# A megakernel's routed expert loops: 23 tiles of 256 slots become 15 of 256 and 9 of 128, written out

## The chip, the cores and the metric

The program runs on one core of one Trainium2 chip. The metric is the device time of one execution in microseconds (us): the median of the runs of a kernel, and for comparisons the ratio to the kernel before on the same chip.

## The reference, cut to what matters

Four decoder layers of mixed kinds run over x of 16 x 128 tokens (2048 tokens) of width 256. The change touches the two layers whose feed-forward part routes each token to 2 of 8 experts:

```python
def moe(x, router_w, router_b, W1, b1, W2, b2, W3, b3):   # layer 0: D_FF = 1024, with biases
    logits = x @ router_w + router_b
    topv, topi = jax.lax.top_k(logits, TOP_K)
    topw = jax.nn.softmax(topv, axis=-1)
    ...
    h = h2 * jax.nn.silu(h1)          # h1 = x W1 + b1, h2 = x W2 + b2
    eo = jnp.einsum('ebsf,efd->ebsd', h, W3) + b3[:, None, None, :]
    return jnp.einsum('bse,ebsd->bsd', comb, eo)
```

Layer 1 has the same form with 512 hidden columns, no biases, sigmoid gating and one more expert that all tokens share. The kernel computes an expert only for the tokens that chose it: 4096 (token, choice) pairs in each of the two layers.

## The kernel before, in words

Each routed stage has two parts. `route` computes the logits, the two choices of each token, and how many tokens each expert has; it gives each pair a slot so that an expert's slots begin at a multiple of `SLOTS` = 256. With 4096 pairs and 8 experts that makes at most `ROUTED` = 23 tiles of 256 slots, 46 chunks of 128. VectorE builds all that in one chain of small steps (`c.step`, `c.wait`: the wait is for all steps before), writes the expert of each tile to `TE`, and, with one-hot matrices (`OA`, `OB`, `OV`) and TensorE, the tables `TOKEN` (which row goes to a slot) and `CHOICE` (where its result goes).

`expert_tiles` then runs over the tiles. A tile has NF chunks of 128 hidden columns, 8 in layer 0 and 4 in layer 1. I call the work on TensorE between `up(t, 0)` and `up(t+1, 0)` the turn of tile t; in it the engine alternates, chunk by chunk (a round), between `up` of tile t and `down` of tile t-1. Each product is made of three single passes (high x high, high x low, low x high) over numbers that are split in a high part of type fp32r and a rest:

- GpSimd (POOL) gathers 2 x 128 rows of a tile with `gather` (an indirect DMA for each 128), three tiles ahead. TensorE transposes them (`turn`), ScalarE and VectorE split them (`CH`, `CL`).
- SyncE (SP) loads a tile's expert weights: `U` (two matrices, 2 MB in layer 0 and 1 MB in layer 1) and `DN` (half as much), each into one of two buffers. For tile t it waits until `UL` of tile t-2 is made, issues `U`, then waits for `DL` of tile t-2 and issues `DN`. The register with the expert's number is loaded first.
- For each chunk ScalarE makes `UH` and `DH` (copies), VectorE makes `UL`, POOL makes `DL` (subtractions). The rings hold 4 chunks.
- `up` has the weights stationary and streams the tile's 256 columns: 12 matmuls of 256 columns for a chunk. `silu` (ScalarE) and `hidden` (VectorE, with bias in layer 0) make `HR`, split again to `HH` and `HL`.
- `down` has `HH`/`HL` stationary and streams 256 columns of `DH`/`DL`: 3 matmuls for each 128 slots, 6 for a chunk.
- The result is copied to `Y` and POOL scatters it with `put`, an indirect DMA for each 128 slots. Offsets for `gather` and `put` are first copied to a small tile `AT`, by POOL and ScalarE.

Each engine's loop is a hardware loop over pairs of tiles (`turns`, line 1464), with the first and the last tiles written out. POOL's order within tile t is DL(0), the copy to `AT`, DL(1), gather of t+3, DL(2) ..., and at chunk `PUT` (4 in layer 0, 3 in layer 1) the put of tile t-1. In layer 0 part of the next layer's keys and values (`kv`) fills TensorE while `route` waits.

Of the kernel before, what the change touches and what calls it, by code (L numbers as in the profile page):

```python
# [39 lines left out]
ROUTED = (2 * T + 8 * (SLOTS - 1)) // SLOTS  # L40


C_IDENT, C_DECAY, C_COS, C_SIN, C_CAUSAL, C_LESS, C_HEAD, C_IOTA, C_END = (
    0, 128, 256, 384, 512, 640, 768, 776, 792)


def shape_constants():
# [15 lines left out]
    c[:, C_IOTA:C_IOTA + 16] = np.arange(16)[None, :]  # L63
    return c
# [16 lines left out]
def build(nc, I, out):  # L81
# [20 lines left out]
    with top:  # L102
# [12 lines left out]
        YT = nc.dram_tensor("results_by_choice", (2 * T + ROUTED * SLOTS, D), F32, kind="Internal").ap()  # L115
# [1008 lines left out]
        def route(tag, RW, bias_rows, gating, gate, W12, ROWS, TAB, TE, expert_tiles, weights, fill=None):  # L1124
# [4 lines left out]
            with ExitStack() as c:  # L1129
# [9 lines left out]
                ST = sb_in(c, f"{tag}_ST", [P, 3, E8])  # L1139
                G = sb_in(c, f"{tag}_G", [P, 3, B])  # L1140
                SL = sb_in(c, f"{tag}_SL", [P, 2, B, E8])
                CMP = sb_in(c, f"{tag}_CMP", [P, expert_tiles, E8 - 1])
                TEF = sb_in(c, f"{tag}_TEF", [P, expert_tiles])
                IOTA_T = sb_in(c, f"{tag}_IOTA_T", [P, expert_tiles])
# [23 lines left out]
                with nc.Block() as block:  # L1168
# [34 lines left out]
                    def _(pool):  # L1203
                        nc.gpsimd.iota(IOTA_T[:, :], pattern=[[1, expert_tiles]], base=0, channel_multiplier=0,
# [34 lines left out]
                    def _(dve):  # L1239
# [42 lines left out]
                        while lag < B:  # L1282
# [6 lines left out]
                        c.step(nc.vector.tensor_scalar(CNT[:, :], SUMS[:, at, B - 1, :], float(SLOTS - 1), None, ALU.add))  # L1289
                        c.wait()  # L1290
                        c.step(nc.vector.tensor_scalar(CNT[:, :], CNT[:, :], SLOTS.bit_length() - 1, None,
                                                       ALU.logical_shift_right))
                        c.wait()
                        c.step(nc.vector.tensor_copy(ST[:, 0, :], CNT[:, :]))
                        c.wait()
                        src, lag = 0, 1
                        while lag < E8:
                            c.step(nc.vector.tensor_copy(ST[:, 1 + (src == 1), 0:lag], ST[:, src, 0:lag]))
                            c.step(nc.vector.tensor_tensor(ST[:, 1 + (src == 1), lag:E8], ST[:, src, lag:E8],
                                                           ST[:, src, 0:E8 - lag], ALU.add))  # L1300
                            c.wait()
                            src, lag = 1 + (src == 1), 2 * lag
                        first_tile = 3 - src
                        c.step(nc.vector.tensor_tensor(ST[:, first_tile, :], ST[:, src, :], ST[:, 0, :], ALU.subtract))
                        c.step(nc.vector.tensor_tensor(SUMS[:, 1 - at, :, :], SUMS[:, at, :, :], sums, ALU.subtract))
                        c.wait()
                        c.step(nc.vector.tensor_tensor(SUMS[:, 1 - at, :, :], SUMS[:, 1 - at, :, :], rank, ALU.add))
                        c.step(nc.vector.tensor_scalar(ST[:, 0, :], ST[:, first_tile, :], float(SLOTS), None, ALU.mult))
                        c.step(nc.vector.tensor_tensor(
                            CMP[:, :, :],  # L1310
                            ST[:, first_tile, 1:E8].rearrange("p (o e) -> p o e", o=1).broadcast_to([P, expert_tiles, E8 - 1]),
                            IOTA_T[:, :].rearrange("p (t o) -> p t o", o=1).broadcast_to([P, expert_tiles, E8 - 1]),
                            ALU.is_le))
                        c.wait()
                        c.step(nc.vector.tensor_reduce(TEF[:, :], CMP[:, :, :], AX, ALU.add))
                        c.step(nc.vector.tensor_tensor(
                            SUMS[:, at, :, :], SUMS[:, 1 - at, :, :],
                            ST[:, 0, :].rearrange("p (o e) -> p o e", o=1).broadcast_to([P, B, E8]), ALU.add))
                        c.wait()
                        nc.vector.tensor_copy(TE[:, 0:expert_tiles], TEF[:, :]).then_inc(s_te, 1)  # L1320
# [8 lines left out]
                        c.step(nc.vector.tensor_copy(SI[:, :, :], G[:, 0:2, :]))  # L1329
                        c.wait()  # L1330
# [14 lines left out]

                        dve.wait_ge(s_tab, 1)
# [16 lines left out]
        class SlotTables:  # L1363


            CHUNKS = ROUTED * SLOTS // P

# [4 lines left out]
        class ExpertWeights:  # L1372


            def __init__(self, c, tag, FF, WUP, WDOWN, TE, bias):
# [3 lines left out]
                if bias:  # L1379
                    self.BU = sb_in(c, f"{tag}_BU", [P, 2, 2, FF // P])  # L1380

# [3 lines left out]
            def expert(self, sp, i, j):  # L1385
                return sp.value_load(self.TE[0:1, bass.ds(2 * i + j, 1)], min_val=0,
                                     max_val=self.WUP.shape[0] - 1)

            def up(self, sp, e, j):
                sp.dma_start(self.U[:, j, :, :, :], self.WUP[bass.ds(e, 1), :, :, :, :]  # L1390
                             .rearrange("o p k a f -> (o p) k a f")).then_inc(self.s_up[j], 16)

            def up_bias(self, sp, e, j):
                sp.dma_start(self.BU[:, j, :, :], self.bias[0][bass.ds(e, 1), :, :, :]
                             .rearrange("o p a f -> (o p) a f")).then_inc(self.s_up[j], 16)
# [12 lines left out]

        def expert_tiles(tag, weights, TAB, fill=None, place=None):

# [2281 lines left out]
```

## Time and profile before

| | us |
|---|---|
| median of 3 runs | 1662.16 |
| lowest and highest | 1660.51, 1671.48 |
| profiled execution, device time | 1667.93 |
| profiled execution, span of the trace | 1666.1 |
| of it TensorE busy | 1401.1 |

The profiled execution is one run. Its device time is 5.8 us above the median, and its span is 1.8 us shorter than its device time; what lies around the span is the start and end of the program. Busy time is the union of an engine's instructions, with modelled ends for matmuls.

### The profile page before, as it was taken

The page shows a single profiled execution, that of the slowest core. Times are in us where ns is not written, and L with a number is a line of the kernel's source. Part 1 is how long each engine was busy: PE and PEld are TensorE (multiplying, and loading weights), DVE is VectorE, ACT ScalarE, POOL GpSimd, SP SyncE. Part 2 cuts the span into 40 slices and gives each one's busy share as a digit, 9 for nine tenths or more (in the row PEclk, how much of TensorE's full clock was granted, in tenths as well). Part 3 has the DMA queues.
Part 4 walks back from the last instruction along what each step waited for, and adds up shares of the span by engine and source line. Part 5 has one row for each costly group of instructions (what it writes and reads, how often), then busy time and mean ns, then how long its engine had stood idle before and what let it go on. Part 6 is the DMA issues. An engine that isn't in the chain of part 4 may idle for free. (4 is left out here: it accounts for less than half of the span.)

```text
span 1666.1 us, 31746 instructions
## 1 busy us (share of the span) xinstructions
PE 1401.1 (84%) x10246; PEld 1189.0 (71%) x10246; DVE 1151.6 (69%) x2497; ACT 939.7 (56%) x2055; POOL 758.4 (46%) x813
## 2 busy tenths in 40 slices
PE   2799978999999999968986579999876976455898
PEld 0445565899999999944665579999875862244787
DVE  6357755688788788756965648778665758786554
ACT  3246642777777777746752338777624546563332
POOL 2223202466666666513321138888701760344444
PEclk8799987999999999979996789999998999675999
DMA  5000005365665665340012117667441000101001
GB/s 178 1 1 1 1 24 200 119 235 190 220 231 189 232 222 189 119 133 1 1 52 89 76 54 234 210 211 228 143 134 60 1 1 0 29 4 59 1 19 33
DMA packets 62367, 171.86 MB, mean 103 GB/s; under 512 B 11760, under 2 KB 43248, under 8 KB 53056
## 3 DMA queue, kind: packets, MB, share of 16 engines
q1 hardware_dynamic: 53440, 146.50, 25.3%
q0 software_dynamic: 8832, 24.13, 4.5%
q8 instruction: 55, 0.90, 0.2%
q14 instruction: 40, 0.33, 0.1%
HBM read 152.25 MB, written 18.35 MB: 102 GB/s over the span
## 5 line engine op out<-in xcount | busy, mean ns | idle before, releaser
L1749 POOL TENSOR_TENSOR l0m_e_DL<-l0m_e_DN,l0m_e_DH 128x256 fp32r<-128x256 f32 x184 | 180.9, 988 | 122.6 <-ACT l0m_e_DH L1588 74.9
L1532 PE MATMUL PS<-l0m_e_CH,l0m_e_UH 128*128 128x256 f32 x736 | 211.3, 287 | 1.9 <-DVE l0m_e_CL L1682 1.9
L1532 PE MATMUL PS<-l0m_e_CH,l0m_e_UL 128*128 128x256 f32 x736 | 209.5, 285 | 0.0
L1532 PE MATMUL PS<-l0m_e_CL,l0m_e_UH 128*128 128x256 f32 x736 | 209.4, 284 | 0.0
L1654 DVE TENSOR_TENSOR l0m_e_UL<-l0m_e_U,l0m_e_UH 128x512 fp32r<-128x512 f32 x184 | 149.0, 810 | 12.1 <-ACT l0m_e_UH L1579 12.1
L1532 PEld LDWEIGHTS PS<-l0m_e_CH,l0m_e_UH 128*128 128x128 f32 x736 | 142.3, 193 | 2.2 <-ACT l0m_e_UH L1579 2.2
L1532 PEld LDWEIGHTS PS<-l0m_e_CL,l0m_e_UH 128*128 128x128 f32 x736 | 142.2, 193 | 0.0
L1532 PEld LDWEIGHTS PS<-l0m_e_CH,l0m_e_UL 128*128 128x128 f32 x736 | 142.1, 193 | 0.0
L1666 DVE SCALAR_TENSOR_TENSOR Z<-PS,l0m_e_BU,Z 128x256 f32<-128x256 f32 x184 | 88.7, 482 | 73.3 <-ACT Z L1596 70.9
L1596 ACT ACTIVATE Z<-PS,l0m_e_BU 128x256 f32<-128x256 f32 x184 | 87.6, 476 | 83.3 <-PE PS L1532 83.3
L1579 ACT CAST l0m_e_UH<-l0m_e_U 128x512 fp32r<-128x512 f32 x184 | 113.0, 615 | 0.0
L1532 PE MATMUL PS<-l1m_e_CH,l1m_e_UH 128*128 128x256 f32 x368 | 107.7, 293 | 5.9 <-DVE l1m_e_CL L1682 5.9
L1548 PE MATMUL PS<-l0m_e_DH,l0m_e_HH 128*128 128x256 f32 x368 | 104.8, 285 | 2.8 <-issue 2.2
L1532 PE MATMUL PS<-l1m_e_CH,l1m_e_UL 128*128 128x256 f32 x368 | 105.1, 286 | 0.0
L1532 PE MATMUL PS<-l1m_e_CL,l1m_e_UH 128*128 128x256 f32 x368 | 105.1, 285 | 0.0
L1548 PE MATMUL PS<-l0m_e_DH,l0m_e_HL 128*128 128x256 f32 x368 | 104.7, 284 | 0.0
L1548 PE MATMUL PS<-l0m_e_DL,l0m_e_HH 128*128 128x256 f32 x368 | 104.6, 284 | 0.0
L1677 DVE TENSOR_TENSOR l0m_e_HL<-Z,l0m_e_HH 128x256 fp32r<-128x256 f32 x184 | 96.8, 526 | 0.1
L1749 POOL TENSOR_TENSOR l1m_e_DL<-l1m_e_DN,l1m_e_DH 128x256 fp32r<-128x256 f32 x92 | 87.1, 956 | 16.0 <-ACT l1m_e_DH L1588 12.7
L1654 DVE TENSOR_TENSOR l1m_e_UL<-l1m_e_U,l1m_e_UH 128x512 fp32r<-128x512 f32 x92 | 79.6, 866 | 21.4 <-ACT l1m_e_UH L1579 20.8
L3443 POOL TENSOR_TENSOR Z<-l3f_WI,Z 128x512 f32<-128x512 f32 x32 | 50.7, 1584 | 60.8 <-DVE Z L3539 55.7
L1532 PEld LDWEIGHTS PS<-l1m_e_CH,l1m_e_UH 128*128 128x128 f32 x368 | 71.5, 194 | 7.6 <-issue 4.9
(545 smaller groups left out, 4509.1 us busy)
## 6 DMA issues: line engine op xcount, KB each, us to landing
l0m_e_U<-in_l_up SPq DMA_DIRECT2D x23, 2048.0 KB
l0m_e_DN<-in_l_down SPq DMA_DIRECT2D x23, 1024.0 KB
l1m_e_U<-in_l_up SPq DMA_DIRECT2D x23, 1024.0 KB, 6.7
l1m_e_DN<-in_l_down SPq DMA_DIRECT2D x23, 512.0 KB, 3.9
CTX<-in_ctx SPq DMA_DIRECT2D x2, 2048.0 KB, 10.0
l1a_GA<-results_by_choice SPq DMA_DIRECT2D x16, 256.0 KB, 5.8
l1m_c_GA<-results_by_choice SPq DMA_DIRECT2D x16, 256.0 KB, 5.0
Z<-in_l_b_rows SPq DMA_DIRECT2D x23, 128.0 KB, 2.3
```

What stands on the lines that cost most here:

```text
L1532: ins = nc.tensor.matmul(hb(f)[:, a * SLOTS:(a + 1) * SLOTS], w[:, f % RING, k, a, :], x[:, j, k, :], start=(p == 0), stop=(p == len(passe ...
L1548: ins = nc.tensor.matmul(yb(j)[:, r * D:(r + 1) * D], h[:, j % 2, f, r * P:(r + 1) * P], w[:, f % RING, :], start=(f == 0 and r == 0 and p ...
L1579: nc.scalar.copy(UH[:, f % RING, :, :, :], U[:, j % 2, :, :, f * P:(f + 1) * P]).then_inc(s_uh, 1)
L1596: nc.scalar.activation(SG[:, f % RING, :], hb(f)[:, 0:SLOTS], ACT.Silu, **kw).then_inc(s_silu, 1)
L1654: nc.vector.tensor_tensor(UL[:, f % RING, :, :, :], U[:, j % 2, :, :, f * P:(f + 1) * P], UH[:, f % RING, :, :, :].bitcast(F32), ALU.subtr ...
L1666: ins = nc.vector.scalar_tensor_tensor(out=HR[:, f % RING, :], in0=second, scalar=BU[:, j, 1, f:f + 1], in1=SG[:, f % RING, :], op0=ALU.ad ...
L1677: nc.vector.tensor_tensor(HL[:, j % 2, f, :], HR[:, f % RING, :], HH[:, j % 2, f, :].bitcast(F32), ALU.subtract).then_inc(s_hl, 1)
L1749: nc.gpsimd.tensor_tensor(DL[:, f % RING, :], DN[:, j, f, :], DH[:, f % RING, :].bitcast(F32), ALU.subtract).then_inc(s_dl, 1)
L3443: nc.gpsimd.tensor_tensor(HR(u), HA(u), HB(u), ALU.add).then_inc(s_h, 1)
```

## The change: what it does

- An expert with n chunks of 128 slots gets n // 2 tiles of 256 and n % 2 of 128. There are 15 wide (B) and 9 narrow (S) tiles, 39 chunks; wide tiles that an input needs beyond 15 become two narrow ones each. All 24 run in a fixed order, BBSBBSBS three times. `route` computes two kinds of starts, two tables of experts and a slot by either kind, so its chain on VectorE is longer; its one-hot matrices have 39 columns in place of 46.
- A narrow tile has the rows stationary and streams 256 columns of weights: 6 matmuls of 256 columns for a chunk, for 128 slots. The output then has slots on partitions, so layer 0's bias comes from a seventh matmul (`PICK`, a one-hot column repeated, times `BROW`), and `HR` is transposed back by TensorE (`turn_hidden`, two transposes for each pair of chunks, a unit). `silu`, `hidden`, `HH` and `HL` take the two chunks of a unit at once. `down` has 3 matmuls for a chunk.
- The hardware loops are gone: all tiles are written out, and `gather` and `put` read the tables without `AT`.
- In layer 0 a 128 x 256 array of biases is loaded and split by POOL ahead of `route`.

```diff
-ROUTED = (2 * T + 8 * (SLOTS - 1)) // SLOTS
+WIDE, NARROW = 15, 9
+ROUTED = WIDE + NARROW
+CHUNKS = 2 * WIDE + NARROW
+TILE_KINDS = "BBSBBSBS" * 3
...
+            units = [(t, f) for t in range(tiles) for f in (range(NF) if big(t) else range(0, NF, 2))]
...
+                if not big(t):
+                    turn_at.setdefault(divmod(NF * t + f + 2, NF), []).append(u)
+                split_at.setdefault(divmod(NF * t + f + (1 if big(t) else 3), NF), []).append(u)
...
-                def turns(eng, body):
-
-
-                    for j in range(2):
-                        body(0, j)
-                    with eng.Fori(1, pairs - 1) as i:
-                        for j in range(2):
-                            body(i, j)
...
+                                half = hb(u)[:, (f % 2) * 2 * P:(f % 2 + 1) * 2 * P]
                                 for p, (w, x, k) in enumerate(passes):
...
+                                    ins = nc.tensor.matmul(half, x[:, t % 2, k, 0:P],
+                                                           w[:, f % RING, k, :, :].rearrange("p a n -> p (a n)"),
+                                                           start=(p == 0), stop=(not bias and p == len(passes) - 1),
                                                            skip_group_check=True)
+                                if bias:
+                                    s = small_index(t)
+                                    ins = nc.tensor.matmul(half, PICK[:, s, f:f + 1].broadcast_to([P, P]), BROW[:, :],
+                                                           start=False, stop=True, skip_group_check=True)
                             ins.then_inc(s_up_done, 1)
...
+                        def turn_hidden(u):
+                            pe.wait_ge(s_hr, u + 1)
+                            for h in range(2):
+                                ins = nc.tensor.transpose(pair(hb(u))[:, h, 0:P], HR[:, u % 4, h * P:(h + 1) * P], IDENT)
+                            ins.then_inc(s_ht, 1)
...
+                        for t in range(tiles + 1):
+                            for f in range(NF):
+                                if t < tiles:
+                                    up(t, f)
+                                if t >= 1:
+                                    down(t - 1, f)
+                                for u in turn_at.get((t, f), ()):
+                                    turn_hidden(u)
+                                if f == NF // 2 and t + 1 < tiles:
+                                    turn(t + 1)
...
+                                up_high(count(t, f) + 2)
+                                down_high(count(t - 1, f) + 2)
+                                for u in split_at.get((t, f), ()):
+                                    hidden_high(u)
+                                if t < tiles and ends(t, f):
+                                    silu(at_unit[t, f])
...
+                                pool.wait_ge(s_dh, count(t, f) + 1)
+                                nc.gpsimd.tensor_tensor(DL[:, f % RING, :], DN[:, t % 2, f, :],
                                                         DH[:, f % RING, :].bitcast(F32), ALU.subtract).then_inc(s_dl, 1)
...
+                                if f == 1 and t + 3 < tiles:
+                                    gather(t + 3)
+                                if f == PUT and t >= 1:
+                                    put(t - 1)
```

## Rows read from the trace of the kernel before

**Rows 1.** The page's head table: busy us, share of the span, instructions.

```profile
PE 1401.1 (84%) x10246; PEld 1189.0 (71%) x10246; DVE 1151.6 (69%) x2497; ACT 939.7 (56%) x2055; POOL 758.4 (46%) x813
```

**Rows 2.** Windows, the two tile loops: length, engines as in Rows 1, PEclk, DMA, GB/s.

```profile
301.00:713.30 412.30, 409.51 (x3400) 408.88 (x3398) 328.47 (x594) 306.59 (x778) 268.50 (x289) 0.99 0.54 195
984.00:1205.50 221.50, 214.60 (x1744) 211.12 (x1744) 171.98 (x296) 161.51 (x431) 184.79 (x197) 0.99 0.62 199
```

**Rows 3.** Timeline of SP's DMA issues in layer 0: start, us, queue.

```profile
399.21 0.33 SPq L1398 DMA_DIRECT2D l0m_e_DN<-in_l_down  x1
400.45 0.34 SPq L1390 DMA_DIRECT2D l0m_e_U<-in_l_up  x1
...
416.93 0.33 SPq L1398 DMA_DIRECT2D l0m_e_DN<-in_l_down  x1
418.48 0.34 SPq L1390 DMA_DIRECT2D l0m_e_U<-in_l_up  x1
```

**Rows 4.** Timeline of PE in layer 0: matmuls one behind another, and a turn.

```profile
407.13 0.28 PE L1532 MATMUL PS<-l0m_e_CH,l0m_e_UH 128*128 128x256 f32 x1
...
408.09 0.28 PE L1532 MATMUL PS<-l0m_e_CH,l0m_e_UL 128*128 128x256 f32 x1
...
519.89 0.60 PE L1516 MATMUL PS<-CONST,l0m_e_ROW 128*128 128x128 f32 x4
```

**Rows 5.** Groups of POOL, layer 1, 1040 to 1183 us: busy, mean ns | idle before.

```profile
L1749 POOL TENSOR_TENSOR l1m_e_DL<-l1m_e_DN,l1m_e_DH 128x256 fp32r<-128x256 f32 x60 | 58.2, 978 | 3.0 <-POOL l1m_e_AT L1723 2.1 <-ACT l1m_e_DH L1588 0.3
L1734 POOL DMA_INDIRECT results_by_choice<-l1m_e_place,l1m_e_AT x30 | 32.6, 1088 | 7.1 <-issue 6.8 <-PE PS L1516 0.3
L1727 POOL DMA_INDIRECT l1m_e_ROW<-rows_by_token,l1m_e_AT x30 | 31.1, 1036 | 6.9 <-issue 6.0 <-ACT l1m_e_place L1618 0.6
L1723 POOL COPY l1m_e_AT<-l1m_TOKEN 128x2 uint32 x14 | 6.9, 490 | 0.0
```

**Rows 6.** Windows of one turn in layer 0, split where the weights have landed.

```profile
399.20:411.00 11.80, 11.80 (x101) 11.80 (x100) 9.31 (x18) 8.74 (x24) 7.73 (x9) 1.00 0.83 300
411.00:416.90 5.90, 5.90 (x52) 5.90 (x51) 5.16 (x9) 4.66 (x12) 4.20 (x5) 1.00 0.13 45
```

**Rows 7.** Waits, layer 1's loop: us in total, times, longest.

```profile
ACT l1m_e_UH L1579 <- DMA l1m_e_U<-in_l_up: 20.7, 14, 3.1
...
PE PS L1532 <- DVE l1m_e_CL L1682: 5.9, 8, 1.5
```

**Rows 8.** Groups of DVE, then ACT, layer 0, 400 to 680 us.

```profile
L1654 DVE TENSOR_TENSOR l0m_e_UL<-l0m_e_U,l0m_e_UH 128x512 fp32r<-128x512 f32 x127 | 103.6, 816 | 0.0
L1677 DVE TENSOR_TENSOR l0m_e_HL<-Z,l0m_e_HH 128x256 fp32r<-128x256 f32 x127 | 66.5, 524 | 0.0
L1666 DVE SCALAR_TENSOR_TENSOR Z<-PS,l0m_e_BU,Z 128x256 f32<-128x256 f32 x127 | 61.2, 482 | 50.8 <-ACT Z L1596 49.1
...
L1596 ACT ACTIVATE Z<-PS,l0m_e_BU 128x256 f32<-128x256 f32 x127 | 60.4, 476 | 58.6 <-PE PS L1532 58.6
```

**Rows 9.** Timeline of layer 0's route: DVE's chain, and the one-hots behind it.

```profile
270.55 0.17 DVE L1289 TENSOR_SCALAR l0m_r_CNT<-l0m_r_SUMS 128x8 int32<-128x8 f32 x1
...
272.05 0.28 DVE L1305 TENSOR_TENSOR l0m_r_SUMS<-l0m_r_SUMS,PS 128x128 f32<-128x128 f32 x1
272.37 0.29 DVE L1307 TENSOR_TENSOR l0m_r_SUMS<-l0m_r_SUMS,PS 128x128 f32<-128x128 f32 x1
...
273.55 0.18 DVE L1320 CAST l0m_TE<-l0m_r_TEF 128x23 int32<-128x23 f32 x1
...
281.54 1.14 DVE L1341 TENSOR_TENSOR l0m_r_OA<-l0m_r_BLK,l0m_r_AB 128x368 bf16<-128x368 f32 x1
...
284.61 0.49 PE L1189 MATMUL PS<-l0m_r_OV,l0m_r_OB 128*128 128x92 bf16 x8 [0.76 <-POOL l0m_r_OV L1215]
```

**Rows 10.** The page's table of DMA issues: KB each, us to landing.

```profile
l1m_e_U<-in_l_up SPq DMA_DIRECT2D x23, 1024.0 KB, 6.7
```

**Rows 11.** The page's DMA queue table, instruction fetches: packets, MB, share.

```profile
q8 instruction: 55, 0.90, 0.2%
```

More of the change, by code:

```diff
@@ L1552, in down @@
                                                            skip_group_check=True)
                             ins.then_inc(s_y, 1)
-                        def tile(i, j):
-                            for f in range(NF):
-                                up(i, j, f)
-                                if begun(i, j, 1):
-                                    down(i, j - 1, f)
-                                if f == NF // 2 and exists(i, j + 1):
-                                    turn(i, j + 1)
                         if fill is not None:
@@ L1564, in _ @@
                             fill.end(pe)
-                        turn(0, 0)
-                        turns(pe, tile)
-                        for f in range(NF):
-                            down(*LAST, f)
+                        turn(0)
+                        for t in range(tiles + 1):
[8 more added lines that the diff above has]
+                                    turn(t + 1)
@@ new lines, in _ @@
+                        up_high(1)
+                        cols_high(0)
+                        for t in range(tiles + 1):
+                            for f in range(NF):
+                                if not bias and f == 1 and t >= 2:
+                                    out_rows(t - 2)
+                                up_high(count(t, f) + 2)
[4 more added lines that the diff above has]
+                                    silu(at_unit[t, f])
+                                if f == NF // 2 and t + 1 < tiles:
+                                    cols_high(t + 1)
@@ new lines, in _ @@
+                        up_low(0)
+                        up_low(1)
+                        cols_low(0)
+                        for t in range(tiles + 1):
+                            for f in range(NF):
+                                up_low(count(t, f) + 2)
+                                if t < tiles and ends(t, f):
+                                    hidden(at_unit[t, f])
+                                for u in split_at.get((t, f), ()):
+                                    hidden_low(u)
+                                if bias and f == 1 and t >= 2:
+                                    out_rows(t - 2)
+                                if f == NF // 2 and t + 1 < tiles:
+                                    cols_low(t + 1)
```

590 lines of the change are left out of this document (310 added, 280 removed).

## The prediction

> **What bounds the kernel now.** The page's head table comes first [rows 1]: TensorE is busy for 84% of the span, more than any other engine, but that is an average over stages. The windows of the two tile loops say more [rows 2]. They are 412.3 and 221.5 us long, 38% of the span, and TensorE is busy for 409.5 and 214.6 us of them at a granted clock of 0.99, the upper of its two levels (2.4 GHz).
>
> Busy time hides how fast the engine steps, so the timeline is next. Matmuls of 256 columns start 0.12 us apart (407.13 to 408.09 with seven between, eight steps of 0.12), though each is shown as 0.28 us long [rows 4]. In layer 0, SP issues `DN` every 17.72 us [rows 3], and that is a turn of TensorE: 144 matmuls x 0.12 = 17.28 us, and 4 transposes for the rest, 0.11 us each. The first and last starts (399.21, 416.93) are one such period, and 23 turns of 17.72 are 407.6 of the 412.3 us. So layer 0's loop is TensorE's alone, with nothing lost at the back edge of the hardware loop.
>
> Layer 1 is another case. Its matmuls and transposes, 1656 x 0.12 + 92 x 0.11 = 208.8 us, leave 12.7 us of the window. POOL's groups between 1040 and 1183 us [rows 5] sum to 128.8 us busy (58.2 + 32.6 + 31.1 + 6.9) and 17.0 idle before them: all 143 us, with overlaps. POOL never waits there for more than a gap. Fifteen tiles in 143 us are 9.5 us each, where TensorE needs 36 x 2 x 0.12 + 0.44 = 9.1. POOL is the second bound, by 5%. Late `DL` holds SP's `DN` issue and the `U` issue behind it, which is where ScalarE's 20.7 us of waits for `U` come from [rows 7].
>
> **Layer 0's loop.** A wide tile keeps its 144 matmuls and 4 transposes. A narrow one has 8 x (6 + 1) for `up`, 8 x 3 for `down`, so 80 matmuls, and 2 + 8 transposes. Before: 23 x 144 = 3312 matmuls and 92 transposes, 397.4 + 10.1 = 407.5 us. After: 15 x 144 + 9 x 80 = 2880 and 78 + 72 = 150, 345.6 + 16.5 = 362.1 us. That is 45.4 us less if TensorE stays the bound. The bias matmul has a stationary operand that repeats one column; no row shows such a load, so I take the 0.12 us of the others. Its bounds are 0 (72 matmuls hidden: 8.6 us better) and the 0.28 of an unpipelined one (72 x 0.16 = 11.5 us worse); all 736 x 3 `up` matmuls of the loop step at 0.12, which is why I take that. For `turn_hidden` the same two bounds lie between 0 and the 0.60 us that four transposes took together with their latency [rows 4], and I stay at 0.11.
>
> What could be late instead in the shorter turns? There are three lengths: wide behind wide 17.7 us, wide behind narrow (120 matmuls) 14.8, narrow behind wide (104 matmuls, 12 transposes) 13.8.
> - *Weights.* `DN` and `U`, 3 MB, move at 300 GB/s and a share of 0.83 in the 11.8 us behind the `DN` issue; in the 5.9 us left of the turn there are 45 GB/s [rows 6]. So they have landed about 10.6 us behind the `U` issue (400.45 to 411). `UH(0)` of the next tile is asked for in round 6 of 8, in a narrow turn 6 x 1.7 = 10.2 us from its start, and `U` is issued about 2 us before that start: 12.2 us against 10.6. It fits, with two more rounds before TensorE itself needs it.
> - *VectorE.* A full round costs it 816 + 524 + 482 ns by mean durations [rows 8], 1.82 us against 1.80 of TensorE where a wide tile follows a narrow one. The window's union is less, 328.5 us for 184 rounds, 1.79 with `CL` and `Y` in it [rows 2]. It sits at the edge in 8 of 24 turns and is idle in the narrow ones (0.82 + half of 1.0 against 1.67), and the rings let it lag by two rounds.
> - *POOL.* 1.02 us a round and four indirect DMAs of 1.3 at most, 13.3 us against 13.8 in the worst turn, 11 to 12 in most.
> I charge 2.5 us for these edges: 43 us saved, 34 to 46 as bounds.
>
> **The new chain in a narrow tile.** TensorE goes from the end of a unit's second `up` to its `turn_hidden` through 19 matmuls in layer 0 (6 + 7 + 6) and 18 in layer 1, 2.2 us. In that time ScalarE makes `silu` (0.48) and VectorE `hidden` (0.48) [rows 8]; in the worst case VectorE has just begun a stretched `UL` (0.82). That is 1.8 us and some 0.2 for four hand-overs, so it is covered by about 0.2 us at worst and by 1 us as a rule. Behind a waiting TensorE would stand the next `up`, and behind that all. Price at zero, up to 0.3 us for half of the 54 units (8 us) as a bound. `HL` of a narrow unit is three rounds late instead of one; `down` needs it a turn later.
>
> **Layer 1's loop.** TensorE: 15 x 72 + 9 x 36 = 1404 matmuls, 78 + 36 transposes, 168.5 + 12.5 = 181.0 us, 27.8 less than 208.8. POOL: a `DL` costs (58.2 + 3.0) / 60 = 1.02 us, an indirect DMA (32.6 + 7.1 + 31.1 + 6.9) / 60 = 1.295, a copy to `AT` 0.49 [rows 5]. Before: 92 x 1.02 + 92 x 1.295 + 23 x 0.49 = 224.2 us. After: 96 `DL` (one tile more), 78 indirect DMAs, no copy: 97.9 + 101.0 = 198.9 us. POOL saves 25.3 us and stays ahead of TensorE's 181 by 10%, so POOL sets this loop and the saving is 25 us. `U`, 1 MB, takes 6.7 us to land [rows 10]; a narrow turn lasts 6.7 and a wide one behind it 7.7 against POOL's mean of 8.3, so the load has as much room as before. Bounds: 35 us if POOL's pace falls away as a bound (181 + the 5 us that every loop has at its end, against 221.5), 10 us if each `U` behind a narrow turn is late by the longest wait seen, 3.1 us [rows 7], at half of the 9.
>
> A rule on POOL bears on this. The rows show `UL` at 816 ns and `HL` at 524 in the mean, both of two SBUF operands, while `hidden` and `CL`, which read PSUM, keep their times; `HL` of a narrow tile reads PSUM. The Trainium skill (GPSIMD Engine Reference, in its table of the engine's facts) says that GpSimd's SBUF interfaces contend with VectorE instructions that have two SBUF inputs. By that rule `DL` gets shorter beside narrow tiles, where half of such work is gone; by the rows alone its mean stays. The sum keeps the mean.
>
> **Loops written out.** Every engine now streams new instructions through both loops. The page shows 55 instruction fetches of 16 KB on one queue, 0.2% of the DMA share [rows 11], and the written-out first and last tiles of layer 0 have the same turn as those inside. I price it at 0; a bound is 1 us for each of some 30 more fetches if none is ahead of its use. The Trainium skill (Runtime: NRT & Kernel Launch, Instruction fetch mechanics) says that a taken branch out of the current window costs a fetch stall and that straight code is fetched ahead. By its first half the loops would gain from the edit; the equal turns of [rows 3] show no such stall to win back.
>
> **Route.** Both routes get a longer chain. From 270.55 to 273.55 there are nine groups of steps with a wait behind each, 3.1 us; a step of 128 x 128 with its wait takes 0.32 (272.05 to 272.37), small ones 0.07 to 0.2 [rows 9]. After it there are fourteen groups, and by the same prices (0.21 + 0.29 + 0.20, three scans of 0.27, then 0.85, 0.75, 0.65, 0.65, 0.45, 0.50, 0.40, 0.40) 6.2 us: 3.1 more. The one-hots shrink by 46 to 39 columns: `OA` at 1.14 us [rows 9] becomes 0.97, three times, and `OV` behind the last, about 0.8 us less in all. The chain ends each route (TensorE waits at 284.61 for it), and layer 0's keys and values come behind it, so 2.3 us more in each: 4.6. Loading and splitting the biases lies beside the transposes ahead of the route: 0. The first `gather` of layer 1 no longer waits for a copy (0.6), and each stage ends in one store fewer; against that I set 1 us for turns that don't average out.
>
> **Sum.** -43 - 25 + 4.6 = -63, and with 3 us for small waits that I have not seen -60. Against the profiled execution, 1667.9 us, that is 1608; it was 5.8 above the median, so against the median of 1662.2 it is 1602.
>
> **Rivals.**
> 1. *Forecast*, 1602 (1592 to 1613), chance 0.55.
> 2. *Layer 1 becomes load-bound and layer 0 VectorE-bound* (the two lower bounds): -34 - 10 + 4.6 = -39, 1623. For it speaks that both rates are within a tenth of their edge; against it that the mean loads leave room. 0.22.
> 3. *POOL lets go*: its `DL` falls to its uncontended time and TensorE sets layer 1: -45 - 35 + 4.6 = -75, 1587. 0.14.
> 4. *The new hand-overs stall TensorE*, slower than before: at each of the 54 units TensorE waits for `silu` and `hidden` because ScalarE or VectorE stands at an earlier wait in its order. It eats the gain from 1.1 us a unit; at 1.5 us it is -60 + 81, 1683. Against it is the cover of 2.2 us. 0.05.
> 5. *No change* (the narrow turns as long as wide ones, because loads take 17 us a tile): the 5.9 us of near idle DMA [rows 6] speak against it. 0.04, 1660.
>
> The predicted time is 1602. The range takes in 1 to 3 and leaves out the last two and the ends: 1584 to 1628. A measurement here tells about 1% (17 us) from no change: faster 0.91, within 1% 0.05, slower 0.04.
>
> **What would show it.** Turns of 17.7, 14.8 and 13.8 us in layer 0 and TensorE still without gaps; in layer 1 POOL without idle time at a mean of 8.3 us a tile; route's chain 2.3 us longer. Wrong would be: waits of PE for `HR` or `UH`, `UL` waits on DMA in layer 0, an instruction fetch in front of a gap, a clock below 0.99 in the loops.

## The result, and the profile after

The changed kernel takes 1604.84 us in the median (1603.77 to 1607.69, 4 runs), against 1666.82 us for the kernel before on the same chip: a ratio of 0.963, with a 95% interval of 0.958 to 0.968. The forecast was 1602; it started from the 1662.16 us of three runs of the kernel before, and a fourth (1675.46) has moved that median. The saving is 62.0 us, where 60 was forecast. The profiled execution took 1603.92 us, its span is 1602.1.

First the page's head table and two of its rows for DMA, those that answer to [rows 1], [rows 10] and [rows 11]; then the windows of the two loops (columns as in [rows 2]).

```profile
PE 1324.1 (83%) x9624; PEld 1110.0 (69%) x9642; DVE 1130.4 (71%) x2469; ACT 906.0 (57%) x1952; POOL 728.4 (45%) x753
...
q8 instruction: 81, 1.33, 0.4%
...
l1m_e_U<-in_l_up SPq DMA_DIRECT2D x24, 1024.0 KB, 6.4
```

```profile
299.10:668.10 369.00, 364.83 (x3026) 363.20 (x3026) 315.55 (x548) 285.70 (x717) 261.41 (x264) 0.99 0.59 224
940.60:1142.00 201.40, 188.57 (x1514) 183.67 (x1514) 158.07 (x273) 149.89 (x392) 160.64 (x168) 0.99 0.64 219
```

The reader is to see two unlike loops. In layer 0 TensorE is still busy for all but 4 us. In layer 1 it is now idle for 13 us of 201, and POOL, which [rows 2] have at 184.8 of 221.5, stands at 160.6 of 201.4: no engine fills that loop. By the starts and ends of the two loops in the trace (first matmul of `up`, last one of `down`) the spans divide like this:

| stretch | before | after | difference |
|---|---|---|---|
| up to layer 0's loop | 300.7 | 299.1 | -1.6 |
| layer 0's loop | 412.6 | 369.0 | -43.6 |
| between the loops | 270.7 | 272.5 | +1.8 |
| layer 1's loop | 221.4 | 201.4 | -20.0 |
| behind it | 460.6 | 460.1 | -0.5 |

So all of the gain is in the loops, 43.6 where 43 was forecast and 20.0 where 25 was.

**Layer 0.** The timeline of PE shows how it steps now (start, us, engine, line, tiles, form):

```profile
332.25 0.28 PE L1588 MATMUL PS<-l0m_e_UL,l0m_e_CH 128*128 128x256 f32 x1
332.37 0.28 PE L1594 MATMUL PS<-l0m_e_BROW,l0m_e_PICK 128*128 128x256 f32 x1
332.49 0.28 PE L1614 MATMUL PS<-l0m_e_DH,l0m_e_HH 128*128 128x256 f32 x1
...
409.09 0.36 PE L1614 MATMUL PS<-l0m_e_DH,l0m_e_HH 128*128 128x256 f32 x1 [0.61 <-issue]
...
409.76 0.29 PE L1614 MATMUL PS<-l0m_e_DH,l0m_e_HL 128*128 128x256 f32 x1
409.88 0.38 PE L1601 MATMUL PS<-CONST,Z 128*128 128x128 f32 x2
410.02 0.36 PE L1588 MATMUL PS<-l0m_e_UH,l0m_e_CH 128*128 128x256 f32 x1
410.22 0.28 PE L1588 MATMUL PS<-l0m_e_UH,l0m_e_CL 128*128 128x256 f32 x1
```

The bias matmul takes a step of 0.12 us like its neighbours, as the forecast priced it. The two transposes of `turn_hidden` (the row of `Z`) cost 0.22 us together, also as priced: the matmul behind them starts 0.14 us after them, but its own step is 0.20 (410.02 to 410.22), so from 409.76 to 410.22 there are 0.46 us, of which two steps of 0.12 are the matmuls'. From the first matmul of each tile to that of the next the trace has 17.49 us for wide behind wide, 15.04 or 14.82 for wide behind narrow, 13.45 for narrow behind wide, and 14.3 where the tile before that wide one was narrow too: there (the 0.89 us from a start at 408.20 to 409.09) TensorE's weight load waits up to 0.8 us for the high part of the down weights.

**Layer 1.** The waits of its loop (us in total, times, longest) answer to [rows 7]; behind them stand POOL's groups from 960 to 1130 us, which answer to [rows 5].

```profile
POOL l1m_e_DL L1812 <- ACT l1m_e_DH L1655: 24.4, 24, 6.6
ACT l1m_e_UH L1645 <- DMA l1m_e_U<-in_l_up: 18.5, 15, 2.5
...
PEld PS L1581 <- ACT l1m_e_UH L1645: 6.3, 5, 1.9
PE PS L1581 <- DVE l1m_e_CL L1755: 6.2, 7, 1.5
```

```profile
L1812 POOL TENSOR_TENSOR l1m_e_DL<-l1m_e_DN,l1m_e_DH 128x256 fp32r<-128x256 f32 x82 | 73.6, 909 | 12.8 <-ACT l1m_e_DH L1655 11.7
L1801 POOL DMA_INDIRECT results_by_choice<-l1m_e_place,l1m_CHOICE x35 | 36.2, 1035 | 7.7 <-issue 7.7
L1792 POOL DMA_INDIRECT l1m_e_ROW<-rows_by_token,l1m_TOKEN x31 | 33.9, 1095 | 6.6 <-issue 5.9
```

POOL now stands idle ahead of `DL` for 12.8 us in this stretch, 11.7 of them waiting for `DH`, so it doesn't set the pace alone. TensorE waits for `CL` and `UH`. Why those are late is seen in the timeline of one start of a tile, all engines:

```profile
1005.02 0.35 SPq L1444 DMA_DIRECT2D l1m_e_U<-in_l_up  x1
```

```profile
1012.47 0.62 ACT L1645 CAST l1m_e_UH<-l1m_e_U 128x512 fp32r<-128x512 f32 x1 [2.14 <-DMA l1m_e_U<-in_l_up]
...
1013.19 0.69 DVE L1720 TENSOR_TENSOR l1m_e_UL<-l1m_e_U,l1m_e_UH 128x512 fp32r<-128x512 f32 x1 [1.74 <-ACT l1m_e_UH L1645]
...
1013.81 0.28 PE L1614 MATMUL PS<-l1m_e_DH,l1m_e_HL 128*128 128x256 f32 x1
1013.88 0.58 ACT L1684 CAST l1m_e_CH<-PS 128x512 fp32r<-128x512 f32 x1
...
1014.69 0.68 DVE L1755 TENSOR_TENSOR l1m_e_CL<-PS,l1m_e_CH 128x512 fp32r<-128x512 f32 x1
...
1015.63 0.36 PE L1581 MATMUL PS<-l1m_e_CH,l1m_e_UH 128*128 128x256 f32 x1 [1.54 <-DVE l1m_e_CL L1755]
```

ScalarE stands at `UH` of the next tile until its weights land (1012.4). TensorE has transposed that tile's rows by 1012.3, but `CH` comes behind `UH`, `DH`, `HH` and `silu` in its order, and VectorE's `CL` behind `UL`, `hidden` and `HL`. TensorE has nothing between 1014.1 and 1015.6. That is the theory of the experiments below: **the order on ScalarE and VectorE, with CH and CL behind the wait for the next weights**. Its rivals are the landing of `U` itself and POOL's pace, which the forecast had taken for the bound.

### The profile page after: what moved, and what is told of

The parts are those of the page before. It is cut to its first block and busy times, and to the rows that moved or that the text cites. A ratio compares the mean times of both kernels' runs of the same rounds, so it can differ in the third digit from the quotient of the medians.

```text
span 1602.1 us, 28284 instructions
## 1 busy us (share of the span) xinstructions
PE 1324.1 (83%) x9624; PEld 1110.0 (69%) x9642; DVE 1130.4 (71%) x2469; ACT 906.0 (57%) x1952; POOL 728.4 (45%) x753
## 5 line engine op out<-in xcount | busy, mean ns | idle before, releaser
L1720 DVE TENSOR_TENSOR l0m_e_UL<-l0m_e_U,l0m_e_UH 128x512 fp32r<-128x512 f32 x192 | 164.5, 862 | 10.7 <-ACT l0m_e_UH L1645 10.4
L1581 PE MATMUL PS<-l0m_e_CH,l0m_e_UH 128*128 128x256 f32 x480 | 138.5, 289 | 2.0 <-DVE l0m_e_CL L1755 2.0
L1581 PE MATMUL PS<-l0m_e_CH,l0m_e_UL 128*128 128x256 f32 x480 | 136.5, 284 | 0.0
L1581 PE MATMUL PS<-l0m_e_CL,l0m_e_UH 128*128 128x256 f32 x480 | 136.4, 284 | 0.0
L1581 PEld LDWEIGHTS PS<-l0m_e_CH,l0m_e_UH 128*128 128x128 f32 x480 | 92.8, 193 | 2.2 <-ACT l0m_e_UH L1645 2.2
L1581 PEld LDWEIGHTS PS<-l0m_e_CL,l0m_e_UH 128*128 128x128 f32 x480 | 92.9, 194 | 0.0
L1581 PEld LDWEIGHTS PS<-l0m_e_CH,l0m_e_UL 128*128 128x128 f32 x480 | 92.7, 193 | 0.0
L1655 ACT CAST l0m_e_DH<-l0m_e_DN 128x256 fp32r<-128x256 f32 x192 | 78.1, 408 | 0.2 <-PE PS L1614 0.2
L1581 PE MATMUL PS<-l1m_e_CH,l1m_e_UH 128*128 128x256 f32 x240 | 71.8, 299 | 7.7 <-DVE l1m_e_CL L1755 6.2
L525 POOL TENSOR_TENSOR l0a_KBD<-l0a_KT,CONST 128x512 f32<-128x512 f32 x32 | 33.4, 1046 | 91.3 <-PE PS L548 62.6
L1645 ACT CAST l1m_e_UH<-l1m_e_U 128x512 fp32r<-128x512 f32 x96 | 59.7, 623 | 24.6 <-DMA l1m_e_U<-in_l_up 18.5
```

Of the source, the lines that this page charges most:

```text
L525: nc.gpsimd.tensor_tensor(KBD[:, h % KR, :, :], KT[:, chunk, b * S:(b + 1) * S].rearrange("p (o s) -> p o s", o=1) .broadcast_to([P, 4, S] ...
L1581: ins = nc.tensor.matmul(hb(u)[:, a * SLOTS:(a + 1) * SLOTS], w[:, f % RING, k, a, :], x[:, t % 2, k, :], start=(p == 0), stop=(p == len(p ...
L1645: nc.scalar.copy(UH[:, f % RING, :, :, :], U[:, t % 2, :, :, f * P:(f + 1) * P]).then_inc(s_uh, 1)
L1655: nc.scalar.copy(DH[:, f % RING, :], DN[:, t % 2, f, :]).then_inc(s_dh, 1)
L1720: nc.vector.tensor_tensor(UL[:, f % RING, :, :, :], U[:, t % 2, :, :, f * P:(f + 1) * P], UH[:, f % RING, :, :, :].bitcast(F32), ALU.subtr ...
```

## The experiments

The move that several of them make is called the early turn: in layer 1 alone, the rows of the next tile are transposed and split in rounds 0 and 1, not in round 2, where ScalarE and VectorE already ask for the next tile's weights. Losses are read from the length of the loops in the trace, since the times of single runs of one kernel differ by up to 22 us. How well such a length repeats is seen where an edit leaves the loop alone: layer 0's loop is 368.9 or 369.0 us in seven traces (after, e3 to e6, e9, e12), and layer 1's is 201.4 in the kernel after and 201.3 in e7. Each kernel has one trace.

**e1_loops_out: the kernel before with its hardware loops written out.**

```diff
-                    with eng.Fori(1, pairs - 1) as i:
+                    for i in range(1, pairs - 1):
```

> The kernel before with its hardware loops written out and nothing else (23 wide tiles, the copies to AT stay). Theory A (the forecast: streaming new instructions costs nothing, the back edge cost nothing): the time of before, within 0.3%, layer 0's loop 412 us with turns of 17.7, layer 1's 221. Rival (instruction fetches are late): 10 to 30 us slower, with gaps in front of TensorE's instructions that nothing else ends. Rival (the back edge and the register arithmetic cost something): 3 us or more faster, layer 1's loop under 218.

1661.8 us, ratio 0.997 (0.994 to 1.001). Layer 0's loop 413.4 (before 412.6), layer 1's 216.0 (before 221.4). So 5 us of layer 1's gain came with this part here, none of layer 0's; e10 and e11 show that they aren't the loops' own cost.

**e2_old_form: the kernel after, but narrow tiles in the wide tiles' form**, weights stationary and 128 columns streamed, no `turn_hidden`, no bias matmul.

```diff
-            big = lambda t: KIND[t] == "B"
+            big = lambda t: True
...
-w[:, f % RING, k, a, :], x[:, t % 2, k, :],
+w[:, f % RING, k, a, :], x[:, t % 2, k, 0:W(t)],
```

> The changed kernel with the 9 narrow tiles in the wide tiles' form: weights stationary, 12 matmuls of 128 columns for a chunk, no turn back, no bias matmul. If a matmul's step goes by its columns (0.06 us for 128): a narrow tile of layer 0 takes 96 x 0.06 + 24 x 0.12 = 8.6 us in place of 10.7, 1 to 2% faster than the changed kernel if ScalarE and VectorE keep up. If the step has a floor near 0.12 us, as a load of 128 columns of weights for each matmul suggests: 14.6 us a narrow tile, layer 0's loop 35 us longer (404), layer 1's up to 19 us longer, 1640 to 1655 us in all. I expect a floor between, 0.08 to 0.12.

1644.66 us, ratio 0.985 (0.979 to 0.991), loops 396.1 (404 expected for a floor near 0.12 us) and 210.0. The timeline of PE in a narrow tile's turn says why half the columns save so little:

```profile
335.62 0.27 PE L1582 MATMUL PS<-l0m_e_CH,l0m_e_UL 128*128 128x128 f32 x1
335.73 0.27 PE L1582 MATMUL PS<-l0m_e_CH,l0m_e_UH 128*128 128x128 f32 x1
335.84 0.27 PE L1582 MATMUL PS<-l0m_e_CL,l0m_e_UH 128*128 128x128 f32 x1
```

A matmul of 128 columns with a new stationary operand takes a step of 0.11 us, where 256 columns take 0.12. What pays is fewer matmuls, and the streamed weights halve those of `up`. That form is worth 27.1 us of the 43.6 in layer 0 and 8.6 of the 20.0 in layer 1.

**e3_up_first: layer 1's SP issues the next tile's `U` ahead of this tile's `DN`.**

```diff
+                        for t in range(2, tiles + 1) if not bias else ():
+                            if t < tiles:
+                                e = weights.expert(sp, t)
+                                sp.wait_ge(s_ul, count(t - 1, 0))
+                                weights.up(sp, e, t)
+                            if t >= 3:
+                                sp.wait_ge(s_dl, count(t - 2, 0))
+                                weights.down(sp, before, t - 1)
+                            before = e
```

> In layer 1 SP issues U of tile t+1 ahead of DN of tile t, so that U no longer stands behind SP's wait for DL, which POOL makes; all else as in the changed kernel. Theory O (POOL's lateness reaches TensorE through SP's order): ScalarE's waits for U (18.5 us) fall to under 6 and layer 1's loop from 201 to 190 to 195 us. Theory P (POOL's own pace sets the loop, by whatever way): it stays at 199 to 203, and waits for DL or DH take the place of those for U. Theory L (the landing of 1.5 MB a tile sets it): 199 to 203 as well, with ScalarE's waits now for DN.

1600.27 us, ratio 0.958 (0.955 to 0.961). Layer 1's loop is 199.1, 2.3 less. `U` lands in 5.1 us in place of 6.4 and ScalarE's waits for it are gone from the list, yet the loop is in the range of theories P and L: `DN` lands in 6.0 us, where it took 3.9, and `CH` now waits for TensorE's transposes instead (20.7 us in the loop).

**e4_no_put_l1: the kernel after without layer 1's 39 scatters**, so that the results of that stage's routed part are not stored.

```diff
-                            if t >= 2:
-                                act.wait_ge(s_store[t % 2], rows_upto(t - 2))
...
                         def put(t):
+                            if not bias:
+                                return
                             pool.wait_ge(s_ycopy, t + 1)
```

> Layer 1's routed results are not stored (its 39 scatters are left out; what the layer adds is then not its experts' output), which takes 39 x 1.3 = 50 us of POOL's work away. Theory P or O (POOL's lateness sets layer 1's loop): it falls from 201 to 186 to 190 us, TensorE's 181 and its end; SP's issues of U come 2 us or more earlier in each tile. Theory L (landing of the weights): it stays above 196.

ScalarE's waits for the stores go with them. 1606.75 us (one run), layer 1's loop 197.6, where 186 to 190 was expected if POOL sets it. POOL is busy for 42 us less and the loop is 3.8 shorter, so in this kernel POOL's pace is a small part of the 20 us by which the loop stands above TensorE's 181.

**e5_turn_first: the early turn.** The condition changes so at three places, for TensorE (round 0), ScalarE and VectorE (round 1):

```diff
-                                if f == NF // 2 and t + 1 < tiles:
+                                if f == (NF // 2 if bias else 1) and t + 1 < tiles:
                                     cols_low(t + 1)
```

> The kernel after the change, with one move in layer 1's loop: the turn of the next tile's second tensors goes to the first round of a tile, and the copies of the combine weights' high and low halves (CH on ScalarE, CL on VectorE) to the second, so that they no longer stand in program order behind the up-cast of the next tile (UH), which waits for its weights to land. In the trace of the kernel after, TensorE starts on the next tile about 3.0 us after its up weights land, and 1.5 us of that is the wait for CL. Theory A (order on ScalarE and VectorE behind the landing is what layer 1 lost against its forecast): about 1.5 us less at each of some seven to ten starts of a tile, layer 1's loop from 201.4 to 188 to 194 us, the whole about 1592 to 1599. Theory B (the landing itself, or GpSimd's pace, sets it): the loop stays at 199 to 203 us, the whole at 1602 to 1607. Layer 0's loop stays at 369 us by both.

1600.0 us, ratio 0.960 (0.956 to 0.963), layer 1's loop 196.8: 4.6 less. The waits of PE for `CL` are gone but for one of 1.5 us, but the gain is less than the 7 to 13 expected. Theory A's range (188 to 194) and theory B's (199 to 203) both missed it; 12 waits of ScalarE for `U` are left between 960 and 1130 us. (The expectation calls `CH` and `CL` parts of combine weights. They are the high and low parts of the next tile's transposed rows.)

**e6_turn_first_up_first: e3 and e5 together.**

> The move of e5 and that of e3 together: CH and CL ahead of the next tile's up-cast, and layer 1's up weights of the next tile issued ahead of the down weights of this one. By theory A both waits at a tile's start are gone and what stays is the down weights' own landing: loop of layer 1 188 to 194 us, the whole 1590 to 1598. If the down weights' landing, which e3 made late, is as costly as the wait that e3 removed, it is e3 again: 199 us, the whole about 1600. Worse than e3 only if both moves delay the down side: 202 us or more.

1594.76 us (1591.45 to 1599.54), ratio 0.957 (0.955 to 0.960), loop 192.7: 8.7 less, more than the 2.3 and 4.6 of the single moves. It has the lowest median of the kernels here that compute everything. It ran on another chip than the kernel after, and the ratios, 0.957 and 0.963, have intervals that overlap (0.955 to 0.960, 0.958 to 0.968), so the gain is shown by the loop and not by the whole time.

**e7_no_bias_mm: the kernel after without the narrow tiles' bias matmul**, so their first products lack the bias.

```diff
-                                if bias:
-                                    s = small_index(t)
-                                    ins = nc.tensor.matmul(half, PICK[:, s, f:f + 1].broadcast_to([P, P]), BROW[:, :],
```

> The kernel after, with the narrow tiles' bias matmul left out (72 in each layer; their tiles' results lack the bias). The forecast priced these at 0.12 us each on TensorE's path in layer 0: 8.6 us, so layer 0's loop goes from 369 to 360 to 361 us, and layer 1's by 0 to 9 us, less than that where weights are waited for. If the loop stays within 2 us of 369, they lay beside other work, and the 43 us of layer 0 are made up otherwise than the forecast had it.

1600.47 us (one run), layer 0's loop 362.5, 6.5 less, not 8.6. Six of the nine turns are 0.7 to 0.9 us shorter (12.57 to 12.73 for 13.45), those of 14.3 by 0.53 only (13.77). TensorE's path pays the 0.12 us of a bias matmul where it isn't waiting for `DH` already; its weight loads wait 2.8 us for `DH` in place of 2.2. Layer 1 has no bias and no such matmul, against what the expectation says; its loop is 201.3, unchanged.

**e8_narrow_last: the 15 wide tiles first, then the 9 narrow ones.**

```diff
-TILE_KINDS = "BBSBBSBS" * 3
+TILE_KINDS = "B" * 15 + "S" * 9
```

> The kernel after, with the 9 narrow tiles behind the 15 wide ones in both loops rather than spread among them. TensorE's work is the same (sum of the turns within 3 us). A narrow tile behind a narrow one offers about 10.7 us of matmuls in layer 0 (80 by 0.12 us and what lies beside) to some 10.6 to 12 us of weights. If spreading them is what hides the weights, layer 0's loop grows by 5 to 15 us to 374 to 384, and layer 1's (6.7 to 7.7 us of matmuls for 9 us or more of transfers in each of nine tiles) by 5 to 20. If the order doesn't matter, both stay within 3 us of 369 and 201.

1612.09 us (one run), loops 375.3 and 205.5: 6.3 and 4.1 more. In layer 0 narrow behind narrow takes 11.1 to 12.0 us for some 10.7 of matmuls and transposes (80 x 0.12 + 4 x 0.22 + 0.22), in layer 1 7.3 to 8.7 for some 5.0. Here is such a start:

```profile
1095.86 0.62 ACT L1645 CAST l1m_e_UH<-l1m_e_U 128x512 fp32r<-128x512 f32 x1 [1.94 <-DMA l1m_e_U<-in_l_up]
1096.38 0.40 ACT L1655 CAST l1m_e_DH<-l1m_e_DN 128x256 fp32r<-128x256 f32 x1
1096.69 0.36 ACT L1684 CAST l1m_e_CH<-PS 128x256 fp32r<-128x256 f32 x1
```

```profile
1097.86 0.36 PE L1588 MATMUL PS<-l1m_e_UH,l1m_e_CH 128*128 128x256 f32 x1 [0.90 <-DVE l1m_e_CL L1755]
```

Spreading the narrow tiles hides weights, and is worth 10 us. In layer 1 the 4.1 us are a little under the 5 to 20 expected: its wide tiles, now all together, run at 9.07 us. Here are twelve of their turns, and POOL's largest group in them:

```profile
966.50:1075.30 108.80, 108.80 (x914) 108.80 (x913) 97.28 (x156) 85.03 (x218) 93.77 (x96) 1.00 0.68 230
```

```profile
L1812 POOL TENSOR_TENSOR l1m_e_DL<-l1m_e_DN,l1m_e_DH 128x256 fp32r<-128x256 f32 x49 | 45.1, 927 | 7.0 <-ACT l1m_e_DH L1655 6.5
```

TensorE has no idle time in them, though `CH` and `CL` stand in the old order. Beside the wide tiles of e1, some of which start late, what is missing here is above all the copies to `AT`. That limits the theory of the order, and comes back with e11.

**e9_expert_early: e5, and SP reads the next expert's number before it waits for `DL`.**

```diff
                                 weights.up(sp, e, t)
+                                if not bias and t + 1 < tiles:
+                                    ahead = weights.expert(sp, t + 1)
```

> The kernel of e5 (CH and CL of layer 1 ahead of the next tile's up-cast), and SyncE reads the next tile's expert number before it waits for DL rather than behind the issue of the down weights. In the kernel after the change, 1.2 to 1.4 us pass between the issue of the down weights and that of the next up weights, the register's load. If the landing of the up weights is what e5 still waits for, the loop of layer 1 gains 0.5 to 1 us in some seven tiles, from 196.8 to 190 to 194 us, and UH's waits for the up weights (14.1 us in e5 from 960 to 1130) fall under 7. If that load is hidden behind the wait for UL, or the transfer takes longer when it begins earlier, the loop stays at 195.5 to 198.

1600.17 us, ratio 0.964 (0.958 to 0.970), loop 196.0. The read is hidden as meant, `U` is issued 0.52 us behind `DN` and no longer 1.1 to 1.4:

```profile
1042.34 0.34 SPq L1455 DMA_DIRECT2D l1m_e_DN<-in_l_down  x1
1042.86 0.33 SPq L1444 DMA_DIRECT2D l1m_e_U<-in_l_up  x1
```

and it buys nothing that can be told from e5 (0.8 us), as the expectation's second case has it, though ScalarE's waits for `U` from 960 to 1130 us fall from 12 (14.1 us) to 7 (10.7 us). Whether the two transfers then share the queues is not shown, since this trace has no landing times; that their order brings `U` in sooner is shown by e3 and e6 (5.1 us).

**e10_wide_turn_first and e11_before_turn_first: the early turn in e1 and in the kernel before itself**, with wide tiles alone; the same three conditions.

> The kernel before with its loops written out (e1) and the move of e5: no narrow tiles. In e1 a turn of layer 1 took 9.07 to 9.14 us in most tiles, which is TensorE's own work, and CH and CL were ready in time. If the order behind the up-cast costs only where narrow tiles make the tiles short, layer 1's loop stays within 3 us of e1's 216 us. If it costs with wide tiles too, it comes to 209 to 212 us, at which every turn is TensorE's 9.07, and then what e5 gained has nothing to do with the narrow tiles.

> The kernel before, hardware loops and all, with the move of e5 alone. The forecast took layer 1's loop of the kernel before (221.5 us) for GpSimd's. If it was, moving CH and CL changes nothing: 219 to 223 us. If TensorE's waits there came from CH and CL behind the landing of the up weights, as e10 found for the written-out loops, the loop falls to 211 to 215 us, and the forecast read the bound of layer 1 wrongly from the start.

One run each, 1656.49 and 1655.88 us, beside 1657.46 and 1668.81 of the kernel before; only the trace is sharp enough here. Layer 1's loop is 212.1 and 212.0 us, and each of its turns behind the first is 9.07. The window of e11 stands for both, with POOL's largest group in it and the one wait of PE that is listed from 990 to 1195 us:

```profile
982.90:1194.90 212.00, 211.01 (x1744) 210.66 (x1744) 180.15 (x296) 162.32 (x431) 174.27 (x197) 0.99 0.64 208
```

```profile
L1749 POOL TENSOR_TENSOR l1m_e_DL<-l1m_e_DN,l1m_e_DH 128x256 fp32r<-128x256 f32 x92 | 78.9, 866 | 18.2 <-ACT l1m_e_DH L1588 14.7 <-POOL l1m_e_AT L1723 2.6
```

```profile
PE PS L1548 <- ACT l1m_e_DH L1588: 0.9, 1, 0.9
```

The move alone takes 9.4 us off the kernel before. So **layer 1 of the kernel before was not bound by POOL's work alone**: its instructions are the same, and the loop runs at TensorE's own pace. But the order alone isn't enough for the loss either, as e8's wide tiles show: there the old order runs at that pace too, with POOL free of its copies. The trace of before fits both. Its turns are 9.07 us at first (tiles 2 to 5), while the start of `DL(0)` slips from 7.4 us behind the start of its turn (tile 2) to 9.6 (tile 7); that tile's turn is 10.80, and none behind it is under 9.16. SP issues each `DN` 0.17 us behind the `DL` that it waits for, and `U` 1.1 to 1.6 us later. So the reading is that POOL's lateness reached TensorE by way of `U`, `UH` and the order behind it, and that either a lighter POOL or the early turn ends it. That the early turn does is shown by e11; that a lighter POOL would is argued from e8, since no run leaves out the copies and nothing else. The hardware loops cost nothing once this is mended (212.0 with, 212.1 without), so e1's 5 us were not theirs: written out, the late starts of tiles were fewer. Why `DL` is shorter there (913 ns against 978), no run tells.

**e12_best_no_put: e6 without layer 1's scatters** (again the routed results aren't stored).

> The kernel of e6, with layer 1's 39 scatters left out (the stage's routed results are not stored). They are some 50 us of GpSimd's time in the loop. If GpSimd's pace is what sets e6's loop of layer 1 (192.7 us), it falls by 5 us or more, towards TensorE's own 181 to 186. If it stays at 190.5 or above, what is left is not GpSimd's but the landing of the weights behind short tiles.

1581.59 us (one run), and layer 1's loop:

```profile
940.70:1126.70 186.00, 183.69 (x1514) 182.51 (x1514) 152.75 (x273) 148.62 (x391) 119.26 (x130) 0.99 0.61 212
```

6.7 us less than e6's 192.7, by its expectation POOL's share. With the order mended, POOL's scatters do hold layer 1 back by that much; in the kernel after the same edit gave 3.8. The turns are now regular, 8.85 us for wide behind wide and all but two of the narrow ones 6.41, which is 48 steps of 0.12 and six transposes of 0.11, TensorE's own work. Between the two profiled executions lie 18 us; 5.3 of the other 11 are in the router's logits (below), and the rest wasn't followed.

## Why the prediction was right, and where it was not

**The forecast's case was right**, and 1604.8 against 1602 is near, but part of that is luck: the forecast took 68 us off the loops, which gave 63.6, and charged 7.6 us elsewhere (4.6 for the routes, 3 for small waits), where the two traces differ by -0.4. The miss and the charge work against each other.

1. *Layer 0, -43: measured -43.6.* TensorE stayed the bound and is idle for 4.2 of 369.0 us. The turns came as forecast within 0.5 us. `turn_hidden` was priced right, 0.22 us a pair. The bias matmul was priced right by step (e7: 6.5 of 8.6 us on the path). The new chain was covered: PE waits for `HR` (which the trace calls `Z` in layer 0 and `place` in layer 1) in neither loop's list, and in layer 0 its weight load does so once, for 0.2 us. Rival 4 fell.
2. *Layer 1, -25: measured -20.0.* This is the weak step, in two places. "POOL sets this loop" was read from a POOL without idle time [rows 5] and a sum that was 5% above TensorE's. That sum, 224.2 us, was longer than the loop itself, and busy time stretches: `DL` took 978 ns in that stretch of before and 869 in e11 (1031 to 1174 us, POOL again without more than gaps), with no edit on POOL. With that the sum becomes 214, of which five gathers lie ahead of the loop and three scatters behind it, so it fits beside TensorE's 212. What the forecast had right is the way by which POOL was felt, late `DL` holding `DN` and `U`. What it missed is the last link, which stood in [rows 7]: PE waiting for `CL`, 8 times, because `CL` stands in order behind ScalarE's wait for `U`. And "the load has as much room as before" failed: in the kernel after TensorE waits 8.5 us for `CL` (5.9 before), and its weight loads 7.1 for `UH` (2.7 before). Of the 15.4 us between the loop's 201.4 and e12's 186.0, the two moves of order are 8.7 and the scatters on POOL 6.7; what is left is five above the 181.0 that the forecast had for TensorE, its allowance for a loop's end. So POOL was a bound in part, and the forecast's 25 from it alone was 5 too much. The 20.0 lies within the stated bounds, 10 and 35 us.
3. *Loops written out, 0: right for what they cost themselves* (e10 against e11). The fetches on that queue rose from 55 to 81, nearly the 30 more that the bound reckoned with, and the repeated turns of layer 0 (17.49, 15.04, 13.45) show no gap for them. The Trainium skill's rule on taken branches (Runtime: NRT & Kernel Launch, Instruction fetch mechanics) shows no stall here, which would stand in the 9.07 of e11; whether the loop's branch leaves the window that the rule speaks of, no run tells.
4. *Route, +2.3 in each: right in layer 0, not told in layer 1.* In layer 0 the chain from `CNT` to the first `SL` step grew from 3.09 to 6.20 us, as worked out, and the one-hots shrank by 0.66 (0.8 forecast), so that the first gather comes 2.4 us later behind `CNT` (19.8 for 17.4 us). In layer 1 the chain grows by the same 3 us, but its first gather comes 5.2 us later behind `CNT`. The 53 to 56 us of mixed work in between vary by 2 to 3 us among the traces of the changed kernels (55.6 after, 53.2 in e4, 52.8 in e6), and that wasn't followed.

```profile
268.13 0.17 DVE L1303 TENSOR_SCALAR l0m_r_CNT<-l0m_r_SUMS 128x8 int32<-128x8 f32 x1
...
274.33 0.49 DVE L1367 TENSOR_TENSOR l0m_r_SL<-l0m_r_OH,l0m_r_SUMS 128x128 f32<-128x128 f32 x2
```

5. *What wasn't in the sum.* The router's logits, the same instructions in both kernels, took 12.4 and 12.3 us before and 10.6 and 9.7 after, 4.4 us less. The windows of that stretch in layer 1, before and after, differ in the granted clock (0.54 and 0.73), a mean between the two levels in both:

```profile
895.00:907.00 12.00, 11.69 (x60) 11.59 (x59) 0.28 (x1) 0.64 (x1) 0.33 (x3) 0.54 0.52 175
```

```profile
848.00:858.50 10.50, 9.69 (x64) 9.62 (x64) 0.29 (x1) 1.42 (x3) 0.96 (x7) 0.73 0.60 200
```

It isn't the change's doing: e1 has 12.2 and 9.8 there, e4 12.4 and 12.3, e6 12.6 and 12.7. Over all fourteen traces the two together take 20.0 to 25.3 us, so before (24.7) stands near the long end and after (20.3) near the short one. Likewise layer 0's loop starts 12.8 us behind its first gather before and 11.2 after, but 12.9 in e3, e6 and e9 and 11.1 in e1. Together these are some 6 us of chance between the two profiled executions, which hide what the routes cost; the 3 us for small waits were an allowance without a row. That is how a layer 1 that fell 5 us short still left the total near the forecast.

The rule on GpSimd's ports that the forecast weighed (the Trainium skill, GPSIMD Engine Reference, table of facts) can't be told apart from the rest here. `DL` did get shorter beside narrow tiles, 978 to 909 ns, but to 913 in e1 and 869 in e11 without any, with VectorE's instructions unchanged.

## What to carry to other kernels

An engine that is busy without a gap is not yet the bound: the same instruction took 978 ns in one kernel here and 869 in another, so test it by moving a rival's wait, or look at what TensorE waited for and in which order the releasing engine had to work. A short step that is ready should not stand in program order behind a wait for a transfer; three moved conditions gave 9.4 us in a loop whose busy numbers named another engine. A loss can need two conditions at once, as a late POOL and that order seem to be here, and then an experiment that takes away one of them doesn't clear the other. When tiles get shorter, the work of an engine is easy to sum, but the room for loads shrinks with every turn: count it at each kind of boundary, and mix short tiles among long ones.

## What the runs showed of the hardware

- With a new stationary operand for each, matmuls of 128 columns (fp32r) start 0.11 us apart and those of 256 columns 0.12: halving the streamed columns saves a twelfth of a step, halving the matmuls half of the steps.
- One instruction of POOL's, `DL` on 128 x 256, took 978, 909, 913 and 869 ns in the mean in the middle of layer 1's loop of the kernels before and after, e1 and e11, and 927 among e8's wide tiles.
- POOL's cast of 128 x 256 to fp32r took 4.30 us, while a subtraction over half of the array took 0.72. POOL's next work came 0.6 us behind the subtraction, so the cast cost nothing here:

```profile
242.86 4.30 POOL L1905 CAST l0m_e_BROW<-l0m_BRAW 128x256 fp32r<-128x256 f32 x1 [5.24 <-DMA l0m_BRAW<-in_l_b_by_chunk]
247.25 0.72 POOL L1907 TENSOR_TENSOR l0m_e_BROW<-l0m_BRAW,l0m_e_BROW 64x256 fp32r<-64x256 f32 x1
```

- SP's read of an expert's number costs 0.6 to 0.9 us between two issues (1.1 to 1.4 us apart with it in the kernel after, 0.52 mostly without it in e9).
- Two transposes of 128 x 128 between such matmuls cost 0.22 us, and the first matmul behind them carries part of it: its step is 0.20 instead of 0.12.
